# The routed experts in pairs of tiles, with the expert weights stationary and the token rows moving

## The reference

```python
logits = flat @ gate_W.T                       # 8 experts
top_v, top_i = top_k(softmax(logits), 2)       # 2 experts for each token
g = silu(einsum('td,edf->etf', flat, w1_e))    # D=128, F=512
u = einsum('td,edf->etf', flat, w3_e)
out_e = einsum('etf,efd->etd', g * u, w2_e)
routed = einsum('te,etd->td', gates, out_e)    # gates: top_v at top_i
shared = einsum(silu(x @ w1_s) * (x @ w3_s), w2_s) / 8   # F=512 in all, for every token
x = x + 0.5 * (0.5 * shared + 0.5 * routed)
```

## Time and profile before

| | |
|---|---|
| median of 3 runs | 769.57 us (766.91 to 769.66) |
| the profiled execution | 770.35 us, its span 768.6 us, mean granted clock 0.969 |
| PE busy | 686.6 us (89%), weight loads 583.7 us (76%) |
| DVE, ACT, POOL busy | 453.1, 336.7, 418.4 us |
| indirect DMAs | 142 fetches, 142 sends |

### The profile page before, as it was taken

The page is one execution under the profiler, slowest core; times in us unless marked ns, Lnnn a source line. Parts: engine busy times, 40 slices in busy tenths (PEclk is TensorE's granted clock), DMA queues, the critical chain, the costliest instruction groups (busy, mean ns, idle before and its releaser), DMA issues.

```text
span 768.6 us, 12871 instructions
## 1 busy us (share of the span) xinstructions
PE 686.6 (89%) x4282; PEld 583.7 (76%) x4282; DVE 453.1 (59%) x1137; ACT 336.7 (44%) x833; POOL 418.4 (54%) x491
## 2 busy tenths in 40 slices
PE   3879849999999999976887777999999999999995
PEld 3667738888888888953664575788888888888883
DVE  6678874444444444447999986884444444444435
ACT  2658412444444444416664526662444444444430
POOL 5600484476676665369997515006367666765330
PEclk9989959999999999999999997999999999999999
DMA  9450011111121111031100000502011112112037
GB/s 311 192 96 16 2 24 34 32 49 46 46 53 46 46 46 42 22 114 54 43 29 1 1 1 24 89 1 50 22 50 49 46 46 52 46 46 42 29 105 247
DMA packets 34782, 43.97 MB, mean 57 GB/s; under 512 B 5984, under 2 KB 27488, under 8 KB 34336
## 3 DMA queue, kind: packets, MB, share of 16 engines
q1 hardware_dynamic: 25632, 24.39, 11.2%
q0 software_dynamic: 9088, 18.78, 9.6%
HBM read 27.47 MB, written 15.66 MB: 56 GB/s over the span
## 4 chain that ended last, share of the span: by engine, by line
PE 68%; DVE 20%; ACT 3%; issue 3%; POOL 2%; DMA 2%; SPq 1%; POOLq 0%; DVEq 0%; ACTq 0%
PE psY L1466 16%; PE psH L1449 8%; PE psG L1307 6%; PE psU L1307 5%; PE psU L1309 5%; PE psG L1309 5%; PE psU L1308 5%; PE psG L1308 5%; PE psH L1378 5%; DVE rec L1063 3%; PE psT L1406 2%; DVE XN L736 2%; DVE hs L746 2%; DVE ln_stats L723 1%; DVE xn L1047 1%
## 5 line engine op out<-in xcount | busy, mean ns | idle before, releaser
L942 DVE SCALAR_TENSOR_TENSOR hr<-silu,gate,psU 128x512 f32<-128x512 f32 x142 | 106.2, 748 | 165.4 <-PE psU L1309 165.4
L639 POOL DMA_INDIRECT results<-yout,target x142 | 139.7, 984 | 114.9 <-DVE yout L968 78.9
L624 POOL DMA_INDIRECT rows<-tokens,source x142 | 137.3, 967 | 101.8 <-DVE source L898 43.5
L1214 ACT ACTIVATE silu<-psG 128x512 f32<-128x512 f32 x142 | 85.0, 598 | 162.6 <-PE psG L1309 162.4
L1466 PE MATMUL psY<-W,hT 128*128 x1120 | 148.0, 275 | 0.0
L1466 PEld LDWEIGHTS psY<-W,hT 128*128 128x128 f32 x1120 | 136.1, 192 | 0.0
L1207 ACT ACTIVATE hT<-psH 128x512 f32<-128x512 f32 x142 | 84.8, 597 | 75.9 <-PE psH L1449 75.9
L1449 PE MATMUL psH<-ident,hr 128*128 128x128 f32 x568 | 85.0, 272 | 0.0
L1449 PEld LDWEIGHTS psH<-ident,hr 128*128 128x128 f32 x568 | 70.6, 140 | 18.6
L1142 ACT ACTIVATE silu<-psG 128x512 f32<-128x512 f32 x64 | 37.9, 594 | 81.7 <-PE psG L1309 61.7
L746 DVE TENSOR_TENSOR hs<-silu,psU 128x512 f32<-128x512 f32 x64 | 43.7, 685 | 46.0 <-PE psU L1309 38.1
(11 more groups left out here) (190 smaller groups left out, 1252.2 us busy)
## 6 DMA issues: line engine op xcount, KB each, us to landing
W<-w_e SPq DMA_DIRECT2D x3, 2048.0 KB, 13.5
tokens<-XN SPq DMA_DIRECT2D x16, 260.0 KB, 6.2
Y<-results SPq DMA_DIRECT2D x32, 128.0 KB, 2.2
YF<-results SPq DMA_DIRECT2D x16, 256.0 KB, 5.8
rows<-tokens,source POOLq DMA_INDIRECT x142, 2.6
results<-yout,target POOLq DMA_INDIRECT x142, 2.3
X<-x SPq DMA_DIRECT2D x8, 256.0 KB, 5.4
out<-X SPq DMA_DIRECT2D x8, 256.0 KB, 2.8
```

The lines of the kernel that those rows point to most:

```text
L624: pool.indirect_dma_start(rows[:, g % RING, t, :], None, tokens, bass.IndirectOffsetOnAxis(ap=source[:, tile:tile + 1], axis=0))\
L639: pool.indirect_dma_start(results, bass.IndirectOffsetOnAxis(ap=target[:, tile:tile + 1], axis=0), yout[:, g % 2, t, :], None).then_inc(y_ ...
L942: dve.scalar_tensor_tensor(hr[:, s.u % 2, :], silu[:, s.u % 2, :], gate[:, s.over(GT) % 2, s.u % GT:s.u % GT + 1], psU[:, s.u % 2, :], ALU ...
L1214: act.activation(silu[:, s.u % 2, :], psG[:, s.u % 2, :], ACT.Silu).then_inc(silu_done, 1)
```

## The change

The unit of routed work becomes a pair of tiles, 256 rows of one expert. Each expert's rows start on a new pair, so there are at most 32 + 7 = 39 pairs, 78 tiles, in 20 groups with two tiles in the last.

```diff
+PT = 2
+PAIR = PT * P
+PAIRS = TOPK * NT // PAIR + E - 1
+RUN = PT * PAIRS
-SEND_LAG = RING + 1
+SEND_LAG = RING + 2
```

```diff
-                    product(psG[:, s.u % 2, :], high, low, W13H[:, 0, cols], W13L[:, 0, cols]).then_inc(g_full, 1)
-                    product(psU[:, s.u % 2, :], high, low, W13H[:, 1, cols], W13L[:, 1, cols]).then_inc(u_full, 1)
+                    if s.u % PT == 0:
+                        pe.wait_ge(pair_weights, PT * (PAIRS * l + s.i // PT + 1))
+                    for out, w, used, full in ((psG, 0, silu_done, g_full), (psU, 1, h_done, u_full)):
+                        pe.wait_ge(used, turn - 1)
+                        for j in range(FT // PT):
+                            f = s.u % PT * (FT // PT) + j
+                            cols, n = slice(f * P, (f + 1) * P), s.u // PT % 2
+                            i = product(out[:, s.u % 2, j * PAIR:(j + 1) * PAIR], w_high[n][:, w, cols],
+                                        w_low[n][:, w, cols], high, low)
+                        i.then_inc(full, 1)
```

```diff
+                def weights_of(p, part):
+                    if p >= PAIRS:
+                        return
...
+                    elif part == 0:
+                        act.wait_ge(u_full, first_routed[l] + PT * (p - 1))
+                    if p not in entries:
+                        entries[p] = act.value_load(w_off[0:1, p:p + 1], min_val=0, max_val=(E - 1) * F)
+                    kept, used = ((W13H, w_high), (W13L, w_low))[part]
+                    act.activation(used[p % 2][:, :, :], kept[:, :, bass.ds(entries[p], F)], ACT.Copy)\
+                       .then_inc(pair_weights, 1)
...
+                for k in range(RUN):
+                    silu_of(Step.of(k, 2), first_routed[l] + k)
+                    if k % PT == 1:
+                        weights_of(k // PT + PT, 0)
+                    elif k > 0:
+                        weights_of(k // PT - 1 + PT, 1)
```

```diff
-                    dve.scalar_tensor_tensor(hr[:, s.u % 2, :], silu[:, s.u % 2, :],
-                                             gate[:, s.over(GT) % 2, s.u % GT:s.u % GT + 1],
-                                             psU[:, s.u % 2, :], ALU.mult, ALU.mult).then_inc(h_done, 1)
+                    half = bass.ds(s.u % PT * (FT // PT), FT // PT)
+                    dve.tensor_tensor(hT[:, s.u // PT % 2, half, :].rearrange("p f c -> p (f c)"), silu[:, s.u % 2, :],
+                                      psU[:, s.u % 2, :], ALU.mult).then_inc(h_done, 1)
...
-                    dve.tensor_copy(yout[:, par, :, :].rearrange("p t d -> p (t d)"), psY[:, :]).then_inc(y_done, 1)
+                    dve.tensor_tensor(yout[:, par, :, :], psY[:, :].rearrange("p (t d) -> p t d", t=GT),
+                                      wide(gate[:, g % RING, :], [P, GT, D]), ALU.mult).then_inc(y_done, 1)
```

Lags grow by two, and out_routed waits at the first tile of a pair until both of the pair's steps are multiplied:

```diff
-                    pe.wait_ge(hT_done, s.i + (RUN * l + 1))
+                    if s.u % PT == 0:
+                        pe.wait_ge(h_done, s.i + (first_routed[l] + PT))
...
-                pipelined(pe, [(in_routed, 2), (look_up, 1), (transpose_h, 3), (out_routed, 4), (transpose_later, 0)],
-                          RUN, 2 * GT, at={3: last_read}, straight=True)
+                pipelined(pe, [(in_routed, 4), (look_up, 5), (out_routed, 6), (transpose_later, 0)], RUN, 2 * GT,
+                          straight=True)
```

More of the change, by code:

```diff
@@ L242, in macaron @@
         gate_parts = sb("gate_parts", [P, 2, GT, TOPK])
[L243 removed]
+        gate = sb("gate", [P, RING, GT])
         found = sb("found", [P, TILES_R])
@@ L273, in macaron @@
         cum = memory["cum"]
-        tile_cmp = memory["tile_cmp"]
+        pair_cmp = memory["pair_cmp"]
         memory = overlaid(
-            [("hr", [P, 2, F], fp32),
-             ("hT", [P, 2, FT, P], fp32),
+            [("hT", [P, 2, FT, PAIR], fp32),
              ("yout", [P, 2, GT, D], fp32)],
             [("XN", [P, TILES, ROW], fp32)])
-        hr = memory["hr"]
         hT = memory["hT"]
@@ L318, in macaron @@
              ("ha", [P, 2, TB * P], fp32)],
-            [("rows", [P, RING, GT, ROW], fp32)],
+            [("rows", [P, RING, GT, ROW], fp32),
+             ("gap", [P, 4 * CH * P - RING * GT * ROW], fp32),
+             ("w_low1", [P, 2, F], fp32r),
+             ("last_chunks", [P, (CHUNKS - 6) * CH * P], fp32),
+             ("w_high0", [P, 2, F], fp32r),
+             ("w_low0", [P, 2, F], fp32r),
+             ("w_high1", [P, 2, F], fp32r)],
             [("XNTL", [P, NT], fp32r), ("XNTH", [P, NT], fp32r)])
@@ L336, in macaron @@
         rows = memory["rows"]
+        w_high = [memory[f"w_high{n}"] for n in range(2)]
+        w_low = [memory[f"w_low{n}"] for n in range(2)]
         psG = ps("psG", [P, 2, 512])
@@ L350, in macaron @@
         ws_split = sem("ws_split")
-        w_high = sem("w_high")
+        high_made = sem("high_made")
         w_split = sem("w_split")
+        pair_weights = sem("pair_weights")
         consts = sem("consts")
@@ L457, in fetched, with slot @@
         def fetched(l, g):
-            whole = l * GROUPS // RING + g // RING + 1
-            short = (l if g % RING == (GROUPS - 1) % RING else 0) + (1 if g == GROUPS - 1 else 0)
-            return 16 * (GT * whole - (GT - LAST) * short)
+            turn = l * GROUPS + g
+            short = sum(1 for n in range(turn % RING, turn + 1, RING) if n % GROUPS == GROUPS - 1)
+            return 16 * (GT * (turn // RING + 1) - (GT - LAST) * short)
+        def slot(l, g):
+            return (l * GROUPS + g) % RING
         def sent(l, par, groups):
@@ L1199, in _ @@
                         cols = bass.ds(part // 2 * WCOLS, WCOLS)
-                        act.activation(W13H[:, part % 2, cols], W13[:, part % 2, cols], ACT.Copy).then_inc(w_high, 1)
+                        act.activation(W13H[:, part % 2, cols], W13[:, part % 2, cols], ACT.Copy).then_inc(high_made, 1)
                     for _ in range(PLAN[l].get(k - 1, 0)):
@@ L1203, in _ @@
                         batches += 1
[L1205 to L1212, removed]
-                        act.wait_ge(h_done, s.i + (first_routed[l] - 1))
-                    act.activation(silu[:, s.u % 2, :], psG[:, s.u % 2, :], ACT.Silu).then_inc(silu_done, 1)
-                pipelined(act, [(silu_routed, 0), (copy_hT, 1)], RUN, 2, straight=True)
+                def weights_of(p, part):
+                    if p >= PAIRS:
+                        return
+                    if part == 0 and p < PT:
+                        act.wait_ge(u_full, shared_at(l, (4 + 2 * p) * FT - 1) + 1)
+                    elif part == 0:
[5 more added lines that the diff above has]
+                       .then_inc(pair_weights, 1)
+                entries = {}
+                act.wait_ge(w_off_done, l + 1)
+                act.wait_ge(w_split, 2 * WPARTS)
+                for p in range(PT):
+                    weights_of(p, 0)
+                    weights_of(p, 1)
+                for k in range(RUN):
[4 more added lines that the diff above has]
+                        weights_of(k // PT - 1 + PT, 1)
                 for k in range(front[l], SHARED):
```

100 lines of the change are left out of this document (40 added, 60 removed).

## The result

The changed kernel takes 748.37 us (median of 4 runs, 746.77 to 750.38) against 768.84 for the kernel before in the same session (766.91 to 769.66): ratio 0.974, 95% interval 0.971 to 0.976, so 20.5 us less. The forecast was 751. The profiled execution took 750.38, with a span of 748.7 where before's was 768.6.

What follows compares the result with a forecast made beforehand. PE's own stream was taken to bound the routed phase. Each layer gains 10.4 us and loses 1.3 at its end: 2 x (10.4 - 1.3) = 18.2 off 770.35 gives 752.1, said as 751; range 744 to 775.

Steps and rivals of the forecast that it cites:

- p = 0.119: PE's routed phase: the distance between two of the new 256-column matmuls would be 0.119 us, forecast range 0.112 to 0.124.
- a price by the column: PE's new matmuls: if the extra over pure streaming goes by the column, they stand 0.117 us apart.
- the prediction's lower bound: PE's new matmuls: weight loads can follow each other at 0.112 us, taken from the fp32 instructions into psY.
- The layer, 190.2: One layer's routed phase on PE: 78 steps, row transposes and an end wait make 190.2 us, against 200.6.
- The end of a layer, +1.3: POOL's six sends behind the last full group's copy: some 1.3 us more on the path in each layer.
- ACT hidden: ACT's weight copies and register load stay hidden beside PE, with 1.56 us left in a pair for the load.
- POOL just hidden, with a floor of about 187.5: POOL's fetches and sends: hidden at 0.119 us a matmul; at 0.112 they keep a layer from going below about 187.5.
- The extra by the load: Rival at PE's new matmuls: the extra goes by the weight load, 0.127 us apart, kernel 766; chance 0.18.
- the shared read path: Rival at PE's new matmuls: loads and moving columns share one read path, 0.140 us apart, kernel 791; chance 0.13.
- ACT's pace: Rival: a 2.2 us register load makes ACT set the pace, PE waits for pair_weights, kernel 801; chance 0.05.
- bare loads: Rival at PE's new matmuls: every weight load stands bare, 0.219 us apart, kernel about 939; chance 0.02.
- POOL's pace: Rival: matmuls at 0.112 us, POOL holds a layer at 187.5, kernel 746; counted within the forecast.

Runs made afterwards that it cites:

- n192: The changed kernel with only 192 of each pair's 256 rows moving through the g and u matmuls; 744.65 us.
- n128: The changed kernel with only 128 of each pair's 256 rows moving through the g and u matmuls; 743.16 us.
- tail: The changed kernel with psY of the last full group copied out and sent in halves, and PE's last two tiles put in psH's bank; 742.98 us, ratio 0.967.
- nocopy: The changed kernel with ACT's weight copies cut to one column of each block from the third pair on, and no table entry loaded; 747.10 us.
- copy4: The changed kernel with ACT's weight copies doubled from the third pair on, the second copy going to an unused buffer; 751.06 us.
- pad: The changed kernel with 640 unused bytes of each partition ahead of the shared part's moving operands, restoring their address in the kernel before; 750.64 us.

## Why the prediction was right

- **What bounds it.** PE's stream in the routed phase, before and after; right. PE had no time left in either, and the other engines waited for it.
- **p = 0.119.** Measured 0.118, and 0.1197 with the placement of before. The number was right, its working only in part. I put it a quarter of the way between a price by the column (0.117) and one by the load (0.127). `n192` and `n128` show that neither holds below 256 columns: there a floor of 0.112 takes over, the prediction's lower bound. The psY rows from which it took that bound couldn't show it by themselves, since their columns alone fill 0.107. The 256 columns by themselves (0.229 / 2 = 0.115) and the floor lie so near each other that little could come of the mistake; that "a quarter of the way" comes out at 0.119 is in part luck.
- **The layer, 190.2.** Measured 189.2, and 191.0 with the old placement, so the forecast lies between the two. Its terms: psY block 0.89 and now 0.88; transposes of rows 0.44 each (the step from 230.46 to 233.21 is 2.75, 0.45 more than 2.30); wait at the end 1.0, measured 0.88.
- **The end of a layer, +1.3.** Measured +0.8. The mechanism is as written: a wait of 0.88 on PE, six sends 1.28 apart behind one late copy. The last send starts 319.82 - 315.10 = 4.72 behind PE's end, where before it was 330.65 - 326.77 = 3.88. The term was 0.5 too large: the last send ends 5.69 behind PE's end, not 6.2. Of that 0.3 is an issue gap (0.30) behind the last send, which its six times 1.28 count and the 331.61 of the kernel before doesn't hold. That the 0.8 reaches the whole time is shown in layer 0 only. `tail` takes the cause away and gets 2.8 us back in layer 0, and 5.4 in all.
- **ACT hidden.** Right (`nocopy`: 189.2 with and without). The margin of 1.56 in a pair was too small, since it added recorded durations. By `copy4`'s distances it is 4.85 - 2 x (0.95 + 0.48) = 2.0. Of that the register load takes 0.61 (`nocopy` against the kernel after), so it stayed hidden with some 1.4 to spare. The Trainium skill (DMA: Bandwidth & Descriptors, Latency and other measured facts) gives such a load about 600 ns, and the trace agrees with its 0.61.
- **POOL just hidden, with a floor of about 187.5.** Right on both sides: it does not hold the kernel after (189.2), and with p at 0.112 the layer stops at 187.2.
- **The rivals.** The extra by the load (p 0.127) and the shared read path (0.140) fall by the measured distance; ACT's pace by the missing waits for pair_weights and by `copy4`; bare loads (0.219) by the measured distance, and by `n192` and `n128`, where fewer columns shortened nothing. POOL's pace comes into force only in `n192` and `n128`.
- **The sum.** 18.2 less was forecast, 20.5 measured. By the phases it is 2 x (11.4 - 0.8) = 21.2, and with `pad`'s placement, on which the prediction was in effect reckoned, 2 x (9.6 - 0.8) = 17.6. Placement is what no step of the prediction held, and that the forecast lies so near both figures is luck to that extent.

## What to carry to other kernels

Read a stream's price from distances between starts, not from durations: both for PE (0.118 where a row says 0.28) and for ACT (0.95 where it says 1.05). A four-byte matmul with a full weight load of its own has a floor of 0.112 us here, so halving 512 columns to 256 costs next to nothing (two at 0.118 for one at 0.231 to 0.233), and anything smaller is paid by the instruction; then count the instructions and the tiles that the new order rounds up. When the engine that bounds a phase gets faster, look at the end of the phase as well: a copy and six sends behind it cost 2.8 us a layer until they were split. And look at whether an untouched stream has changed its pace: part of a gain, or of what an experiment seems to price, can be placement.

## What the runs showed that I had not expected

- The place of the operands in SBUF changes the distance of untouched matmuls from 0.233 to 0.229 (512 columns) and from 0.1197 to 0.118 (256), together some 2.5 to 3.6 us; 640 unused bytes, with no other edit, bring it back.
- Consecutive ACT instructions overlap by about 0.1: copies of 1024 columns recorded with 1.05 start 0.95 apart, a silu recorded with 0.59 lets the next one start after 0.48.
- 128 and 192 moving columns cost the same 0.112, while bf16 matmuls of 156 columns, each with its own load, come every 0.07.
- A register load takes 0.61 us of ACT behind a wait that has only just ended, and nothing that shows when ACT has work before it.
